# Second experts in order of their number of rows, in slots of falling size

## The reference, cut to what matters

```
scores = sigmoid(xf @ gate_w.T)                  # 8192 tokens, 64 experts
top_scores, top_idx = top_k(scores, 2)           # two experts a token, 16384 pairs
top_scores = top_scores / top_scores.sum(-1) * 2.5
buf[e, pos] = x of the pair, for pos < 512       # an expert takes 512 rows at most
h = silu(buf @ w1[e]) * (buf @ w3[e])            # 256 -> 128
y = h @ w2[e]                                    # 128 -> 256
routed = sum over the two pairs of y * top_score
x = x + shared expert + routed
```

## Time and profile before

| | us |
|---|---|
| median of three runs | 2105.18 (2103.22 to 2107.63) |
| the profiled execution | 2106.05, its span 2104.2 |
| second experts, first issue to last scatter | 1658 to 2029 |
| sums of the results after them | to 2104 |

### The profile page before, as it was taken

The page is one execution under the profiler, slowest core; times in us unless marked ns, Lnnn a source line. Parts: engine busy times, 40 slices in busy tenths (PEclk is TensorE's granted clock), DMA queues, the critical chain, the costliest instruction groups (busy, mean ns, idle before and its releaser), DMA issues. The chain is left out here.

```text
span 2104.2 us, 38489 instructions
## 1 busy us (share of the span) xinstructions
PE 1910.8 (91%) x12194; PEld 1439.0 (68%) x12194; DVE 1509.8 (72%) x3332; ACT 1247.3 (59%) x1870; POOL 1070.3 (51%) x1266
## 2 busy tenths in 40 slices
PE   7999999992999999996689999999896899999996
PEld 6899888882888888886244454444443588878854
DVE  5777778753666666665589899889987477766659
ACT  4444444431666666665588878877775277767630
POOL 3355565533333333332655766767742377777740
PEclk9999999995999999999799999999998899999998
DMA  7444544214455555554424222123220255555559
GB/s 305 152 176 178 181 179 153 81 41 148 150 179 190 171 170 182 176 180 135 168 70 137 86 95 93 65 94 125 95 84 4 90 187 186 178 173 180 188 210 360
DMA packets 138148, 315.42 MB, mean 150 GB/s; under 512 B 36990, under 2 KB 67808, under 8 KB 133952
## 3 DMA queue, kind: packets, MB, share of 16 engines
q1 hardware_dynamic: 106560, 271.77, 38.4%
q0 software_dynamic: 31488, 42.39, 5.8%
HBM read 206.67 MB, written 151.56 MB: 170 GB/s over the span
## 5 line engine op out<-in xcount | busy, mean ns | idle before, releaser
L1906 DVE TENSOR_TENSOR c_att<-c_p_s,adj 128x1024 f32<-128x1024 f32 x256 | 300.3, 1214 | 55.5 <-PE c_p_s L1409 55.5
L1701 ACT ACTIVATE c_att<-c_att 128x1024 f32<-128x1024 f32 x256 | 268.7, 1056 | 117.6 <-DVE c_att L1906 110.7
L995 POOL DMA_INDIRECT moe_y<-b_y,b_goal x144 | 156.1, 1084 | 328.1 <-DVE b_y L1047 294.2
L2228 POOL DMA_INDIRECT moe_y<-d_y,d_goal x256 | 259.9, 1015 | 114.2 <-issue 54.4
L154 PE MATMUL b_p_y<-b_w2h,b_hh 128*128 128x256 f32 x576 | 169.4, 294 | 8.8 <-DVE b_hl L160 3.9
L476 POOL DMA_INDIRECT moe_in<-a_xn,a_rows x128 | 141.5, 1106 | 57.5 <-issue 28.9
L160 DVE TENSOR_TENSOR b_hl<-b_ht,b_hh 128x512 fp32r<-128x512 f32 (+1 forms) x160 | 101.6, 639 | 88.3 <-ACT b_ht L1153 88.3
L155 PE MATMUL b_p_y<-b_w2l,b_hh 128*128 128x256 f32 x576 | 160.8, 279 | 0.0
L156 PE MATMUL b_p_y<-b_w2h,b_hl 128*128 128x256 f32 x576 | 160.8, 279 | 0.0
L1365 POOL DMA_INDIRECT moe_in<-c_xn,c_rows x128 | 131.1, 1025 | 53.1 <-issue 37.8
L1422 PE MATMUL c_p_o<-c_att,c_xp 128*32 128x512 f32 x1024 | 139.0, 615 | 6.1 <-ACT c_att L1701 3.7
(11 more groups left out here) (273 smaller groups left out, 5736.3 us busy)
## 6 DMA issues: line engine op xcount, KB each, us to landing
b_w<-in_moe_w SPq DMA_DIRECT2D x80, 512.0 KB, 4.2
moe_in<-b_zeros SPq DMA_DIRECT2D x65, 520.0 KB, 11.0
d_xin<-moe_in SPq DMA_DIRECT2D x64, 520.0 KB, 3.6
adj<-in_adj SPq DMA_DIRECT2D x32, 1024.0 KB, 5.6
b_xin<-moe_in SPq DMA_DIRECT2D x32, 520.0 KB, 5.7
c_g<-moe_y SPq DMA_DIRECT2D x32, 512.0 KB, 6.1
moe_y<-c_zeros SPq DMA_DIRECT2D x32, 512.0 KB
d_w<-in_moe_w SPq DMA_DIRECT2D x64, 256.0 KB
```

Of the source, the lines that this page charges most:

```text
L995: pool.indirect_dma_start(out=m["moe0_y"], out_offset=bass.IndirectOffsetOnAxis(ap=goal[:, h, t:t + 1], axis=0), in_=y[:, h, t, :], in_off ...
L1701: act.activation(part, part, ACT.Tanh).then_inc(att_ready, 1)
L1906: dve.tensor_tensor(att[:, u % 2, 2 * c:2 * c + 2, :], p_s[:, 2 * c:2 * c + 2, :], adj[:, h, u % T, :].unsqueeze(1).broadcast_to([P, 2, N] ...
L2228: pool.indirect_dma_start(out=m["moe1_y"], out_offset=bass.IndirectOffsetOnAxis(ap=goal[:, h, t:t + 1], axis=0), in_=y[:, h, t, :], in_off ...
```

## The change

The 64 experts run in 64 slots. Slots 0 and 1 hold experts 0 and 1 and keep 512 rows; slots 2 to 63 hold the other 62 in falling order of their number of rows. Slot s has room for 16384/(s - 1) rows, 512 at most, in three or four tiles of n partitions, n rounded up to a multiple of 4. `slot_shape` gives n and tiles: 128 x 4 up to slot 33, then 124 x 4 down to 100 x 4 in slots 34 to 43, and 128 x 3 down to 88 x 3 in slots 44 to 63. Every transposed, converted, multiplied and scattered piece takes that size; the weights keep theirs. Slots 2 to 31 stay in a loop, slots 32 to 63 are written out. VectorE makes the table at the start of the stage; TensorE turns the ranks into a list by one product with the experts' numbers. SyncE reads expert and first row from it ahead of each load. In the attention stage a semaphore is merged into another.

```
+def slot_shape(s):
+    if not isinstance(s, int) or s < FIXED:          # FIXED = 2
+        return P, T
+    most = min(CAP, 2 * TOK // (s - FIXED + 1))
+    tiles = T if most > (T - 1) * P else T - 1
+    return 4 * -(-most // (4 * tiles)), tiles
+
+def slots(eng, body):
+    body(0, 0, True, False)
+    body(0, 1, False, False)
+    with eng.Fori(1, FULL_PAIRS) as q:               # FULL_PAIRS = 16
+        body(q, 0, False, False)
+        body(q, 1, False, False)
+    for q in range(FULL_PAIRS, E1 // 2):
+        body(q, 0, False, False)
+        body(q, 1, False, q == E1 // 2 - 1)
...
             def load_rows(q, h):
-                sp.dma_start(xin[:, h].rearrange("p t d -> p (t d)"), rows_in[2 * q + h]).then_inc(s_rows[h], 16)
+                n, tiles = slot_shape(2 * q + h)
+                row = 0 if at_start(q) else sp.value_load(table[0:1, 1, bass.ds(2 * q + h, 1)], min_val=0,
+                                                          max_val=(E1 - 1) * CAP)
+                at = slice(h * CAP, (h + 1) * CAP) if at_start(q) else bass.ds(row, n * tiles)
+                sp.dma_start(xin[0:n, h, 0:tiles].rearrange("p t d -> p (t d)"),
+                             m["moe1_in"][at, :].rearrange("(p t) d -> p (t d)", p=n)).then_inc(s_rows[h], 16)
+
+            def weights_of(q, h):
+                if at_start(q):
+                    return a["moe1_w"][h]
+                e = sp.value_load(table[0:1, 0, bass.ds(2 * q + h, 1)], min_val=0, max_val=E1 - 1)
+                return a["moe1_w"][bass.ds(e, 1)].rearrange("e p c -> p (e c)")
...
+            def rank_experts():
+                dve.scalar_tensor_tensor(out=place[:], in0=m["count1"][:], scalar=float(E1), in1=iota,
+                                         op0=ALU.mult, op1=ALU.subtract).then_inc(rank_step, 1)
...
+                dve.tensor_tensor(own_place[:], place[:], ident[:, 0:E1], ALU.mult).then_inc(rank_step, 1)
...
+                dve.tensor_reduce(ours[:], own_place[:], AX, ALU.add).then_inc(rank_step, 1)
...
+                dve.tensor_scalar(above[:], place[:, FIXED:E1], ours[:, 0:1], None, ALU.is_gt).then_inc(rank_step, 1)
...
+                dve.tensor_reduce(rank[:], above[:], AX, ALU.add).then_inc(rank_step, 1)
...
+                dve.tensor_scalar(chosen[:], iota[:, 0:RANKED], rank[:, 0:1], None, ALU.is_equal)\
...
+            pe.matmul(p_y[0:1, 0, 0:RANKED], m["consts"][0:E1, C_OWN:C_OWN + 1], chosen[0:E1, :],
+                      start=True, stop=True).then_inc(rank_step, 1)
...
-            act.activation(cdh[:], cd[:], ACT.Copy).then_inc(cd_split, 1)
+            act.activation(cdh[:], cd[:], ACT.Copy).then_inc(init, 1)
```

More of the change, by code:

```diff
@@ L55, with scattered_before @@
 EPS = 1e-5
-C_ID, C_TRI, C_ONE, C_IOTA, C_THR, C_BLK, C_TOK, C_END = np.cumsum([0, P, P, P, E1, NTHR, NBLK, T])
+C_ID, C_TRI, C_ONE, C_IOTA, C_THR, C_BLK, C_TOK, C_OWN, C_END = np.cumsum([0, P, P, P, E1, NTHR, NBLK, T, 1])
+FIXED = 2
+RANKED = E1 - FIXED
+FULL_PAIRS = 16
 DW = D + 4
 W1_1, W3_1, W2_1, W_END1 = np.cumsum([0, KD * H1, KD * H1, D])
-def pairs(eng, n, body):
-    body(0, 0, True, False)
[L69 to L78, removed]
+def slot_shape(s):
[5 more added lines that the diff above has]
+def slots(eng, body):
+    body(0, 0, True, False)
+    body(0, 1, False, False)
[5 more added lines that the diff above has]
+        body(q, 1, False, q == E1 // 2 - 1)
+def scattered_before(q, h):
+    if not isinstance(q, int):
+        return 16 * T * q
+    return 16 * sum(slot_shape(2 * i + h)[1] for i in range(q))
 def each_block(eng, body):
@@ L2029, in moe1_and_sums_phase @@
         arrived_ready, goal_ready = sem("arrived_ready"), sem("goal_ready")
-        rows_in = m["moe1_in"].rearrange("(e p t) d -> e p (t d)", p=P, t=T)
+        place = sb(ctx, "d_place", [P, E1])
+        own_place = sb(ctx, "d_own_place", [P, E1])
+        ours = sb(ctx, "d_ours", [P, 1])
+        above = sb(ctx, "d_above", [P, RANKED])
+        rank = sb(ctx, "d_rank", [P, 1])
+        chosen = sb(ctx, "d_chosen", [P, RANKED])
+        table = sb(ctx, "d_table", [1, 2, E1], I32)
+        rank_step = sem("rank_step")
+        CHOSEN, ORDERED, TABLED = 6, 7, 9
         later = sb(ctx, "d_later", [P, len(LATER), KD, N])
@@ L2080, in _ @@
                 load_down(0, h)
-            pairs(sp, E1, one)
+            sp.wait_ge(rank_step, TABLED)
+            own_wait(sp, mark_sp)
+            slots(sp, one)
             for i in range(NLATER):
@@ L2125, in one @@
                 e = 2 * q + h
+                n, tiles = slot_shape(e)
+                c = slice(0, n * tiles)
                 pe.wait_ge(xl_ready, e + 1)
@@ L2208, in _ @@
             split_in(0, 0)
-            pairs(act, E1, one)
+            slots(act, one)
             result(E1 // 2 - 1, 1)
@@ L2226, in one @@
                     own_wait(pool, mark_pool)
[L2227 removed]
+                    for t in range(2 * c, min(2 * c + 2, tiles)):
                         pool.indirect_dma_start(
[L2229 to L2230 removed]
+                            out=m["moe1_y"], out_offset=bass.IndirectOffsetOnAxis(ap=goal[0:n, h, t:t + 1], axis=0),
+                            in_=y[0:n, h, t, :], in_offset=None, bounds_check=2 * TOK - 1, oob_is_err=False)\
```

99 lines of the change are left out of this document (68 added, 31 removed).

## The result

| | before | after |
|---|---|---|
| median of the runs | 2104.2 us (2101.13 to 2107.63) | 2118.2 us (2115.67 to 2122.12) |
| ratio to before | | 1.0062, 95% interval 1.0047 to 1.0077 |
| span of the profiled execution | 2104.2 | 2120.3 |

What follows compares the result with a forecast made beforehand. The prediction took a ScalarE and VectorE ring of 5.33 us a slot as the bound, three rings just below. Terms -3.2 + 1 - 21.8 + 19 - 6 = -11.0 gave 2095.0 us profiled, 2094.2 median; range 2074 to 2111.

Steps and rivals of the forecast that it cites:

- Step 3: Row loads whose partitions 16 does not divide: equal shares, so 124, 116, 92 use four engines; +19 us, bounds 12 to 25.
- Step 1: Fewer rows in slots 34 to 63: scatters stay 1.29 us apart, slots 34 to 44 gain 3.2 us, short-slot rings at most 4.15.
- Step 4: End of the stage: last xh to last scatter shrinks from 21.3 us to 15.3, -6 us.
- Step 2: Three table reads a slot on SyncE: +1 us in full slots; short slots take 4.4 us, -21.8 us.
- the ring through the reads on SyncE: Short slots: table reads delay row and weight loads, giving rings of 4.3 and 4.25 us a slot; 4.4 taken.
- the ScalarE and VectorE ring of step 1: Conversions, weight splits and y in turn: 5.34 us a full slot, 4.11 with 320 rows and three tiles.
- Step 5: Ranking before the first xl, some 3 us, hidden by VectorE's idle time; merged semaphore nothing; straight code taken as 0.
- Late rows in the loop: Rival: long reads ahead of row loads use up the spare, full slots take 5.6 us; +8, 2102; chance 0.18.
- Even division: Rival: row loads of any partition count stay evenly shared, the 19 us term goes; 2075; chance 0.20.
- TensorE's clock: Rival: gaps in TensorE's work drop its clock to the 1.2 GHz level in short slots; 2112; chance 0.12.

Runs made afterwards that it cites:

- the second experiment: Only the row loads widened to a multiple of 16 partitions, against the changed kernel; tiles, products and scatters unchanged: 2091.65 us, ratio 0.9938.
- the last experiment: Slot 34 alone given 124 partitions, against the kernel with sizes rounded up to multiples of 16: 2091.36 us, ratio 0.9933.
- the sixth experiment: First block of sums put before the shared expert's second gate, against the kernel with sizes of 16 and early table reads: 2083.19 us, ratio 0.9889.
- the third experiment: Experts in the order of their numbers, without table reads, against the changed kernel, same sizes: 2111.99 us, ratio 1.0042.

## Why the prediction was wrong

*Step 3, the term that was mis-sized.* "I take equal shares, because a transfer cut by partitions is simplest so" was right, as was the rule. The size, +19, was not: undoing the division gives back 26.6 us (the second experiment). Slot 34 alone was forecast at a landing of 8.1 and +3.95; the landing was 8.1 and the slot cost 5.8 (11.1 from xh to xh). Slot 35 was forecast at +1.1 and cost 5.5. The working saw such a load as a time of its own with a spare of 4.15 before it. It left out what the load does to others: scatters issued beside it land after 7 us instead of 3.8 (the chain above, and the idle 6.04 in the last experiment), their buffers hold d_goal, and by the order of VectorE and SyncE the next rows leave late. That the scatters land late because they share the four engines is the likely reason; no row shows a single engine. So loads of a pair do not share a spare: the rows of slots 35 and 46 left at 1850.88 and 1929.46, after those of 34 and 45 had landed at 1850.04 and 1928.29. In 48 and 49 and in 61 and 62 the second still left before the first had landed. The changed kernel against the second experiment, trace by trace, says where the term was short: 5.0 us up to slot 34 for 3.95, 12.1 in slots 34 to 44 for 4.7, and 9.6 in 44 to 63 for 10.25. The bound named in the text, 12 to 25, is passed by a little.

*Step 1, the scatter, a price outside its bounds.* It took 1.29 us for any number of partitions, with 1.13 as the lower end and 1.29 as the upper. Measured in the changed kernel, from start to start where no wait lies between: 128 partitions 1.29, 112 and 96 1.25, the others 1.30 to 1.32, but 124, 116 and 92 1.62, 1.57 and 1.48. With 1.62 GpSimd needs 6.5 us a slot. Sizes of 16 in all parts against sizes of 16 in the loads alone: 6.7 us. That the scatters make all of this difference is not shown, since products and conversions change their sizes too; but those get longer with 16, and in the kernel with only the loads widened GpSimd stands idle for more than 0.31 us once between 1900 and 1953 (2.25 before 1930.74). No term of the prediction had this. Nor did the -3.2 of slots 34 to 44 come: with sizes of 16 they take 0.6 less than before, with the loads alone widened 1.2 more.

*Step 4 failed.* "-6" was to come from the last scatter, which is 3.6 us nearer to the last xh (17.8 for 21.4). The end did not follow; it lies 98.6 us after that xh for 97.2. TensorE's last product of the experts comes 1.4 us earlier (11.8 after the last xh for 13.2), and from it to the end are 86.8 us for 84.0, 84.8 to 86.4 in the kernels with sizes of 16. The last scatter had a spare already before the change. VectorE's first sum stands behind gates of the shared expert that wait for TensorE, 18.8 us after TensorE's last product of the experts, and does not wait for its loads, which SyncE issued at 2030.51, 8.5 us earlier. With scatters of 124 alone the last scatter comes 7 us later in the stage and its loads go out at 2099.48; only there does the first sum wait for them. Before, and then with scatters of 124:

```profile
2038.98 3.25 DVE L2303 SCALAR_TENSOR_TENSOR x<-adj,gate,x 128x256 f32<-128x256 f32 x8
```

```profile
2104.68 3.25 DVE L2303 SCALAR_TENSOR_TENSOR x<-adj,gate,x 128x256 f32<-128x256 f32 x8 [2.26 <-DMA adj<-moe_y]
```

From issue to use are 5.2 us there, so before the change some 3 us were spare, and an earlier last scatter could not bring the first sum forward. Behind the first sum the sums are bound by their own traffic and by VectorE, as the rows had it: DMA share 1.00 and VectorE 19.83 of 20 in 2060 to 2080. The earlier first sum of the sixth experiment gave nothing either. Why these 84 us became 86 is open.

*Step 2 was right in size, in part by luck, and not in its cause.* Short slots take 4.43 us with sizes of 16, for 4.4; -21.2 us in slots 44 to 63 for -21.8. But the ring through the reads on SyncE, which was to decide, does not set it: with the issues 0.6 apart it stays 4.44. Most short slots come at 3.9 to 4.4, the mean is raised by some of 4.6 to 5.6, mainly among the first ones with 384 rows, where the ScalarE and VectorE ring of step 1 alone gives 5.34 - 0.69 - 0.19 = 4.46. The reads were priced well, SyncE's issues 1.2 to 1.5 us apart and full slots at 5.34. The reads, kernel after:

```profile
L2093 SPq TENSOR_LOAD <-d_table x124: 263/274/790, 1670.5 to 2021.1; - x124
L2084 SPq TENSOR_LOAD <-d_table x62: 263/271/439, 1669.3 to 2017.1; - x62
```

Behind waits they can have cost something only where a late load makes each issue part of the path (the third experiment is 4 to 6 us shorter without them, with other things changed).

*Step 5 was right.* VectorE at the stage's start, kernel after: the ranking ends at 1662.5 and the first xl, at 1667.27, has waited for its rows since.

```profile
1660.16 0.22 DVE L2299 SCALAR_TENSOR_TENSOR d_place<-count,consts 128x64 f32<-128x64 f32 x1 [0.89 <-PEq L1183]
...
1662.32 0.20 DVE L2316 TENSOR_SCALAR d_table<-d_p_y 1x62 int32<-1x62 f32 x1
1667.27 1.22 DVE L177 TENSOR_TENSOR d_xl<-d_p_tr,d_xh 128x1024 fp32r<-128x1024 f32 x1 [4.74 <-ACT d_xh L2237]
```

The 1.8 us at the start of the stage stand between the two traces at 977 us already, before the first changed instruction (c_cdh, 1005.8), and the experiments start the stage between 1655.8 and 1660.2.

*The rivals.* Late rows in the loop: not seen, 5.34 a slot. Even division: excluded by 4 landing records. TensorE's clock: it appeared, for short times, around waits for rows. Kernel after, windows over slots 34 and 35:

```profile
1840.00:1850.00 10.00, 4.53 (x27) 3.79 (x25) 4.24 (x10) 4.62 (x10) 6.75 (x7) 0.97 0.33 90
1850.00:1860.00 10.00, 8.08 (x32) 6.85 (x32) 4.42 (x9) 4.44 (x8) 4.43 (x5) 0.68 0.35 88
1860.00:1867.00 7.00, 5.17 (x21) 4.35 (x22) 2.12 (x3) 2.40 (x4) 3.58 (x4) 0.76 0.53 138
1867.00:1874.00 7.00, 6.44 (x45) 5.83 (x43) 4.97 (x11) 4.60 (x9) 3.16 (x4) 1.00 0.30 83
```

TensorE in order of time, same kernel, in the third window:

```profile
1863.61 0.61 PE L171 MATMUL d_p_h<-d_xh,d_wh 128*128 128x496 f32 x1
1864.03 0.61 PE L172 MATMUL d_p_h<-d_xl,d_wh 128*128 128x496 f32 x1
```

Products of 496 columns start 0.42 us apart there, the level of 1.2 GHz. Before the change, at a granted 1.00, those of 512 columns start 0.23 apart:

```profile
1828.23 0.39 PE L156 MATMUL d_p_h<-d_xh,d_wl 128*128 128x512 f32 x1
1828.46 0.39 PE L154 MATMUL d_p_h<-d_xh,d_wh 128*128 128x512 f32 x1
```

From slot 34 to the last xh the stretches at a granted 0.50 add up to 27 us, so at most 14 us were lost to them, much of it in slots that waited for rows anyway. They are mainly a consequence of the late loads: with sizes of 16 the granted clock is 1.00 in both stretches shown, and with the loads alone widened it fell once (0.97 over 1892 to 1990). Their own share of the 26.6 us was not separated.

In sum, by the experiments: the rest of the change is worth -20 us (2084.95, ratio 0.9904), loads on four engines cost 26.6, the remaining odd sizes 6.7; 2105 - 20 + 27 + 7 = 2119 for the measured 2118.2. Against the forecast the profiled execution is 27 us off (16.1 later instead of 11.0 earlier). The table above has 11.8 of them in slots 34 to 44, 6.7 in 44 to 63, 7.4 behind the last xh and 1.8 ahead of slot 2. By cause these are 7.6 of the loads beyond the 19, 6.7 of the other odd sizes, which no term had, and the 7.4 of step 4; the rest is small and open. The version to keep is the one with sizes of 16; early reads and an early sum (ratio 0.9889 for both) can't be told from it.

## What to carry to other kernels

Choose partition counts of a DMA as multiples of 16; counts of 124, 116 and 92 in nine of the slots, with the other odd ones, cost 33 us here, more than the 20 us that the smaller tiles gave. When a transfer gets slow, ask not only for its own spare but which other transfers land late beside it, and whose wait stands ahead of the next issue. Before a gain at the end of a stage is counted, look at what the next stage waits for first and what it is bound by then: a share of 1.00 gives nothing back for an earlier start.

## What the runs showed of the hardware that was not expected

- An indirect scatter on GpSimd with fewer partitions can take longer: 1.62 us apart with 124 for 1.29 with 128, shown alone in a kernel that changed nothing else. The dear counts, 124, 116 and 92, are the ones whose row loads had 4 landing records. They also make more packets: with 124 everywhere the profile counts 56064 packets on the software queue, which the scatters use, for 31488 before, 96 more for each of the 256 scatters, at 42.7 MB for 42.4. Whether it is these that take GpSimd's time was not tested.
- A scatter of GpSimd is hit by a row load with 4 landing records beside it: it landed after 7.05 us instead of 3.3 to 3.8.
- A read of a number from a table on the chip takes 271 to 274 ns at the median on SyncE (263 at the least), and three of them a slot, ahead of waits or behind, leave no trace in the time when the loads are not late.
